# Styled self-attention start-up on one NeuronCore: style and key work reordered among VectorE, GpSimd, ScalarE and TensorE

## What is computed

```python
def modulated_linear(x, s, aff_w, aff_b, w, b):
    style = s @ aff_w.T + aff_b
    w_mod = w[None, :, :] * style[:, None, :]
    demod = rsqrt(sum(w_mod * w_mod, axis=2) + EPS)
    w_mod = w_mod * demod[:, :, None]
    return einsum("bni,boi->bno", x, w_mod) + b
kx = modulated_linear(x, s, k_aff_w, k_aff_b, k_w, k_b)      # 16 heads of 32
scores = einsum("bnhd,bnjd->bnhj", kx, kx) / sqrt(32)        # heads against heads of one token
out = einsum("bnhj,bnjd->bnhd", softmax(scores), kx)
x = x + modulated_linear(out, s, o_aff_w, o_aff_b, o_w, o_b)
...
h = silu(s @ W1 + b1) @ W2 + b2     # three small MLPs on the conditions, used by the last layer
w = softmax(aw)
```

## Time and profile before

| | us |
|---|---|
| median of 3 runs (993.44 to 996.03) | 995.06 |
| the profiled execution's own time | 994.71 |
| its span in the trace | 992.9 |
| PE busy | 969.8 (98%) |
| POOL busy | 698.5 (70%) |
| DVE busy | 664.8 (67%) |
| ACT busy | 501.5 (51%) |
| mean granted TensorE clock | 0.991 of 2.4 GHz |

### The profile page before, as it was taken

One profiled execution on the slowest core, in us unless ns is written; L12 is line 12 of the kernel. 1 busy time (PEld: TensorE's weight loads), 2 busy tenths in 40 slices (PEclk: granted clock), 3 DMA queues, 4 the chain that ended last, 5 costly groups with the idle time before them and its releaser, 6 DMA issues.

```text
span 992.9 us, 18147 instructions
## 1 busy us (share of the span) xinstructions
PE 969.8 (98%) x6539; PEld 774.3 (78%) x6539; DVE 664.8 (67%) x1215; ACT 501.5 (51%) x791; POOL 698.5 (70%) x634
## 2 busy tenths in 40 slices
PE   8999999999999999999999999999999999999995
PEld 5567777777777678888888888888888888888884
DVE  6798767689878778666566667657557557565542
ACT  3789878787887555333333343433334334323332
POOL 5557666676675559887777778778768768777861
PEclk7999999999999999999999999999999999999998
DMA  9654654564423562342243143332332233232220
GB/s 279 222 161 139 236 198 151 175 214 147 148 80 95 183 223 75 104 148 95 67 122 120 67 130 103 117 110 80 114 111 72 83 105 121 67 100 100 80 78 22
DMA packets 58557, 125.11 MB, mean 126 GB/s; under 512 B 8051, under 2 KB 12533, under 8 KB 57444
## 3 DMA queue, kind: packets, MB, share of 16 engines
q1 hardware_dynamic: 46692, 82.00, 24.6%
q0 software_dynamic: 11776, 41.95, 13.6%
HBM read 105.98 MB, written 17.95 MB: 125 GB/s over the span
## 4 chain that ended last, share of the span: by engine, by line
PE 75%; POOL 9%; issue 6%; DVE 5%; DMA 2%; ACT 2%; SPq 0%; POOLq 0%; DVEq 0%; ACTq 0%
PE ps L625 37%; PE ps_k L694 7%; PE ps_y L632 7%; PE ps_o L632 6%; PE tp L637 5%; PE ps_v L666 2%; PE ps_s L711 2%; PE ps_u L743 1%; PE tp L972 1%; PE ps_t L756 1%; PE ps_z L960 1%; PE ps_vt L704 1%; DMA path_rows<-in_path,pid 1%; POOL h L1938 1%; POOL om L1868 1%
## 5 line engine op out<-in xcount | busy, mean ns | idle before, releaser
L1924 POOL TENSOR_TENSOR rstd<-var_eps,half 128x1 f32<-128x1 f32 x95 | 54.6, 574 | 95.6 <-DVE var_eps L1672 94.9
L1281 ACT ACTIVATE g_out<-ps 128x512 f32<-128x512 f32 x31 | 18.5, 597 | 163.4 <-PE ps L1077 163.4
L1678 DVE TENSOR_SCALAR shift_n<-mean_var,rstd 128x1 f32<-128x1 f32 x96 | 20.5, 214 | 97.2 <-POOL rstd L1924 95.1
L1868 POOL TENSOR_TENSOR om<-om,bc 128x512 f32<-128x512 f32 x32 | 41.4, 1295 | 62.1 <-DVE om L1426 61.9
L1094 ACT ACTIVATE at_diag<-at 32x512 f32<-32x512 f32 x128 | 80.3, 628 | 7.3 <-DVE at L1458 5.8
L1855 POOL TENSOR_SCALAR xb<-xb,bias_o 128x512 f32<-128x512 f32 x32 | 54.8, 1713 | 40.9 <-DMA xb<-in_x_wide 40.8
L1094 ACT ACTIVATE k_diag<-kt 32x512 f32<-32x512 f32 x128 | 80.1, 626 | 1.1
L1232 ACT ACTIVATE h<-h,shift_n,rstd 128x512 f32<-128x512 f32 x32 | 26.1, 816 | 82.8 <-DVE shift_n L1678 82.8
L1658 DVE TENSOR_TENSOR t_lo<-tp,t_hi 128x512 fp32r<-128x512 f32 x64 | 43.8, 684 | 28.9 <-ACT t_hi L1228 28.9
L1986 POOL DMA_INDIRECT path_rows<-in_path,pid x32 | 41.9, 1309 | 19.5 <-POOL pid L1974 19.5
L694 PE MATMUL ps_k<-wk_hi,xh 128*128 128x512 f32 x128 | 54.7, 430 | 0.7 <-DVE xl L1477 0.7
(11 more groups left out here) (334 smaller groups left out, 3188.8 us busy)
## 6 DMA issues: line engine op xcount, KB each, us to landing
raw<-in_dec_w SPq DMA_DIRECT2D x30, 512.0 KB, 5.4
x_in<-in_x_turned SPq DMA_DIRECT2D x32, 256.0 KB, 5.1
xb<-in_x_wide SPq DMA_DIRECT2D x32, 256.0 KB, 4.3
x_dram<-xb SPq DMA_DIRECT2D x32, 256.0 KB, 3.9
xt<-x_dram SPq DMA_DIRECT2D x8, 1024.0 KB, 8.4
out<-o SPq DMA_DIRECT2D x31, 256.0 KB, 2.1
raw<-in_int_W SPq DMA_DIRECT2D x7, 1024.0 KB, 6.1
id_rows<-in_id_rows SPq DMA_DIRECT2D x32, 64.0 KB
```

What stands on the lines that cost most here:

```text
L1868: nc.gpsimd.tensor_tensor(om[:, :], om[:, :], bc[:, STYLE_O, t // TB, :], ALU.mult).then_inc(mix_step, 1)
L1924: nc.gpsimd.tensor_tensor(rstd[:, k:k + 1], var_eps[:, k:k + 1], half[:, :], ALU.pow).then_inc(norm_step[k], 1)
```

## The change

It does the following, all within the first stages.

1. `keep_busy` makes six unused products instead of five ahead of the styles, and three instead of two behind them.
2. POOL squares two chunks of W_k instead of three; DVE squares chunk 2 and chunk 3, and makes the styles between the two, ahead of the low parts of chunks 1 and 2. The low part of chunk 3 goes from DVE to POOL, behind the scaling of x tile 0 and ahead of the demodulation's power.
3. PE's first three products wait for W_k's high parts only; the low parts are waited for at the rest of them (as before).
4. On DVE the demodulation's `vareps_ko` goes ahead of the two mask copies.
5. On ACT the Silu's table is loaded by a one-column Silu (`first_silu`), then the first key's four diagonal copies are written, then comes the MLP's Silu. Before, the diagonals stood behind the Silu, the second `bc`, and the Exp of `aw` with its table load. That Exp goes from `prepare(0)` to the end of `prepare(1)`.
6. In stage 1 DVE makes `xl` of tile 2 ahead of the transpose to `kt` of tile 1, not behind it.

```diff
-            keep_busy(ps_o, 5)
+            keep_busy(ps_o, 6)
...
-                    keep_busy(ps_o, 2)
+                    keep_busy(ps_o, 3)
                     pe.wait_ge(style_step, 3)
                     pe.wait_ge(square_ready[0], C)
                     row_sum(w_sq[0]).then_inc(squares_step, 1)
-                    pe.wait_ge(wsplit_lo[0], C)
+                    pe.wait_ge(wsplit_hi[0], C)
...
-                if has(1):
...
+                if has(1) and s > 1:
+                    diagonal_key(s - 1)
...
                 if s == 1:
                     ...
+                    act.wait_ge(aw_step, 2)
+                    nc.scalar.activation(aw_exp[:, :], aw_low[:, :], ACT.Exp).then_inc(aw_step, 1)
...
                         if b == 0:
+                            act.wait_ge(demod_bc_ready, 1)
+                            nc.scalar.activation(first_silu[:, :], bc[:, DEMOD_K, 0, 0:1], ACT.Silu)
+                            diagonal_key(0)
                             act.wait_ge(mlp_step, 2)
                             nc.scalar.activation(mlp_h1[0:MLP_ROWS, :], mlp_h1[0:MLP_ROWS, :], ACT.Silu).then_inc(mlp_step, 1)
-                    act.wait_ge(aw_step, 2)
-                    nc.scalar.activation(aw_exp[:, :], aw_low[:, :], ACT.Exp).then_inc(aw_step, 1)
...
             split_low(0, 0)
+            square_k(2)
+            style_of(0, ps_first, 1)
+            square_k(3)
             split_low(0, 1)
-            style_of(0, ps_first, 1)
-            dve.wait_ge(wk_in[C - 1], 16)
-            nc.vector.tensor_tensor(w_sq[0][:, C - 1, :], ...)
             split_low(0, 2)
-            split_low(0, 3)
...
+                if s == 1:
+                    x_low(s + 1)
                 if has(0):
...
-                if has(-1):
+                if has(-1) and s != 1:
+                    x_low(s + 1)
...
-            for c in range(C - 1):
+            for c in range(2):
                 pool.wait_ge(wk_in[c], 16)
...
                 if s == -1:
+                    pool.wait_ge(wsplit_hi[0], C)
+                    nc.gpsimd.tensor_tensor(wk_lo[:, C - 1, :], w_raw[0][:, C - 1, :], wk_hi[:, C - 1, :].bitcast(F32),
+                                            ALU.subtract).then_inc(wsplit_lo[0], 1)
                     pool.wait_ge(squares_step, 4)
```

30 lines of the change are left out of this document (17 added, 13 removed).

## The result

| | before | changed |
|---|---|---|
| median of 19 runs each, us | 995.18 (993.44 to 997.01) | 997.25 (996.18 to 1000.27) |
| ratio | | 1.0024 [1.0017, 1.0031] |
| profiled execution, its own time / span | 994.71 / 992.9 | 1000.27 / 998.5 |

The change makes the kernel 2.1 us slower. The forecast was 994.3, in a range up to 995.8: wrong in sign and outside the range. The ratio, with its 95% interval in brackets, is an estimate of its own over all runs and not the quotient of the two medians.

A forecast was written before the change was run, and what follows sets the result against it. PE was taken as the bound, its full stretch starting when stages 2 to 8 allow; x tile 3's landing cut the first tiles' 2.0 to 5.6 us to 0.7. From 994.71 that gives 994.0, plus 0.35 for the median 994.3; range 992.0 to 995.8.

The forecast's parts named there:

- Nothing is lost: Start-up, unused products: the sixth delays the styles up to 0.85 us, to about 8.6, before DVE asks at about 8.8.
- The anchor: Stage 2, POOL: x tile 3's transfer fixes its scaling until 36.43; `e` follows directly, 0.69 us earlier than 37.12.
- Rival B: Whole start-up gain gets through with the clock at 2.4 GHz: some 3 to 4.4 us, 990.7 to 991.7; chance 0.11.
- Rival A: x tile 3's transfer lands at 34.0, 1.35 us sooner; gain 2.0 us, total 992.7; chance 0.16.
- Rival D: PE's gaps between 33 and 42 us make its clock fall; slower, 996.7 to 999.1; chance 0.05.
- The row sums: Start-up, PE: they start at about 10.2, 0.6 us earlier, with bounds of 0.3 and 0.9.
- PE's gap ahead of them: Start-up, PE's wait before the row sums: the 2.1 us gap shrinks to under 0.5 us.
- The low part on POOL: Start-up: POOL's low part takes 1.04 to 1.49 us, ends by about 12.8, and costs nothing.
- `rinv` ready near 31.4: Tile 0's softmax: with a clock that stays up, 4.4 us are won and `rinv` is ready near 31.4.

The follow-up runs named there:

- unshifted: Changed kernel with `first_silu` allocated behind all other tensors, so nothing else moves; 995.79 us against 994.82 before, ratio 1.0009.
- unshifted_few: unshifted with five and two unused products, as in the kernel before, instead of six and three; 995.13 us against 994.82 before, ratio 1.0000.
- before_raw_shifted: Kernel before with an unused one-column tensor moving only raw W_k, W_o and their squares by 32 bytes; 995.22 us against 994.76, ratio 1.0006.
- unshifted_x3_first: unshifted with x tile 3's transfer issued ahead of the last second MLP weight; 995.58 us against 994.76 before, ratio 1.0010.
- after_128: Changed kernel with `first_silu` 32 columns wide, so tensors behind it move by 128 bytes; 996.70 us against 994.31 before, ratio 1.0025.
- before_many: Kernel before with six and three unused products instead of five and two; 994.89 us against 994.82 before, ratio 1.0003.
- aligned: Changed kernel with `first_silu` 16 columns wide, 64 bytes a partition in place of 32; 996.31 us against 995.37 before, ratio 1.0014.
- before_cut: Kernel before with its unused products cut into six of 213 columns and three of 171; 996.80 us against 994.76 before, ratio 1.0019.

## Why the prediction was wrong

**What failed first: the term that was not in the sum.** The forecast prices six edits and passes over the line that allocates `first_silu`: it puts that at nothing without a word. It is the dearest line of the change. By the ratios: changed 1.0024, without the move 1.0009, a difference of 1.5 us; the kernel before with the move alone 1.0023, 2.3 us. Moving `oh`, `ol` and `xb` alone gives 1.0013, 1.3 us of it. What the rest comes from was not separated.

**"Nothing is lost" for the unused products.** The step priced PE's time ahead of the styles, and said that whether they hold the clock changes nothing of the total. The clock did hold in the profile (1.00 at 9 to 10 and 19 to 20 us), and something was lost all the same, at a place 380 us later, through eight more instructions: POOL waits for the gather 1.92 us in unshifted and 0.74 in unshifted_few, and the ratios are 1.0009 and 1.0000. The order of PE's list was the same there; its place in code blocks wasn't. The size in the total, about 1 us, rests on two pairs whose intervals touch.

**The anchor was right; its gain is not shown in the total.** Forecast: `e` immediately behind x tile 3's scaling at 36.4, `kt` of tile 2 at 38.8. unshifted has 36.47 and 38.78, unshifted_few 38.23. The gain behind it passed to tile 31 (0.71 and 0.88 us of 0.66 and 1.21). But these are gains over a profile of before whose clock fell. The same instructions with a clock that stays up come to 38.03 (before_raw_shifted), against the same anchor. The forecast took its 0.69 us from that one profile and did not ask how far the median already has them. With both side effects taken out, unshifted_few gives 1.0000 where the forecast's sum was 0.9993; the interval, 0.9991 to 1.0009, holds both, so the 0.7 us are neither shown nor excluded. Rival B is excluded by the same rows and by unshifted_x3_first, which got through only with the transfer moved. Rival A's landing at 34.0 didn't come: x tile 3 is scaled from 34.71 to 35.81 in the kernels that keep its place in the queue and have products at 389 to 390. What came ahead of 35.38, up to 0.67 us, lies within the forecast's bounds.

**Rival D, at another place.** I put PE's dry gaps at 33 to 42 and gave them 0.05. A gap that cost the clock came at 23.9 us, because PE arrived early at tile 1's products while `xl` of tile 1 hung, through `kt` of tile 0 and the key bias, on a transfer that POOL's wait counts without needing it. I had called that stretch free and never asked what `kt` of tile 0 waits for once PE is not the last. It cost 5.5 us for 12 products in place of 3.2 in the changed kernel's profile. It is in the profiles of changed, unshifted and after_128, but not in before_many or aligned, and unshifted_few shows no loss: it is a hazard of single executions and was not separated in the median. The time itself, 997.25, lies in rival D's span of 996.7 to 999.1; that is luck, since D's fall of the clock between 33 and 42 us did not come, and the dearest line was not in it.

**Small terms.** The row sums were forecast at 10.2 and start at 10.67 in the changed profile, whose chunks of W_k landed up to 0.7 us later; in seven of the other eleven profiles with the new order they start at 9.67 to 9.87, sooner than my bound. PE's gap ahead of them was to be under 0.5 us and is 1.74 in the changed profile and 0.87 in unshifted_few. The low part on POOL took 1.72 us, above my bound of 1.49, and it was not free: DVE's own low part beside it took 1.76 us in place of 0.68, and PE waited 0.36 us for `xl` of tile 0. For a clock that stays up I had `rinv` ready near 31.4; in the six profiles of the new order with a clock that did, and one semaphore for the biases, it is ready at 33.6 to 34.5. Two sums are off and change nothing: two of ten records of 4.63 us are 0.93 us and not 0.85, and 4.4 us less than 994.7 is 990.3 and not 990.7.

The Trainium skill (GPSIMD Engine Reference, Engine selection) calls GpSimd about two times slower; by that I estimated 1.4 us for the low part. The measured 1.72 us is 2.5 times DVE's 0.68 alone, and no slower than DVE's 1.76 at the same time.

**The range.** It left nothing for costs outside the first 60 us, on the ground that PE's stretch from there is full. But where an engine is full, every product that takes 5 ns longer delays the end.

## What to carry to other kernels

Allocate a new tensor last, or check which addresses an edit moves, and compare the mean duration of the main products in a stretch where TensorE never waits: an unused one-column tensor cost as much as the whole change. When instructions are added ahead of a long unrolled list, look far behind them for a wait on a gather that got longer, and treat the count as something to tune. Before a gain is read off a single profile, look whether its clock is the usual one of that kernel. And before making an engine early, list every wait that its next input stands behind, semaphores that count more than is needed included.

## What the runs showed of the hardware

- Products of 128x512 whose moving operand lies 32, 64 or 128 bytes further took 391 to 396 ns instead of 389 to 390, in eight profiles of eight, and 389 to 390 in all twelve where it stayed. The rule behind the address is open; alignment to 64 or 128 bytes isn't it.
- A 16 KB packet of TensorE's code took 0.96 us of one DMA engine in the kernel before. Where it came 0.25 to 1.5 us behind the first packet of a gather, the wait for the gather was 1.89 to 2.30 us (7 profiles); where it came 2.0 to 2.25 us behind, 0.57 to 0.84 (9 profiles).
- The same pause of TensorE costs its clock in one execution and not in the next: ahead of tile 1's mixing it pauses 1.86 us in before and in before_cut alike; in before the clock stays at 2.4 GHz and tile 5's `kt` follows tile 4's by 7.91 us, in before_cut it falls (0.61 from 61 to 62) and that takes 9.09. With gains and losses of 1 to 2 us this is much of the spread of the runs.
